# Slots in four operations with the sum of the ranks in PSUM, and new orders of the engines, in an attention and mixture-of-experts kernel

## The reference

```python
def _L0_attn_ref(x, w_qkv, w_swiglu, w_out):
    qkv = jnp.einsum('btd,ed->bte', rms_norm(x), w_qkv)
    q, k, v = jnp.split(qkv, 3, axis=-1)
    q = rms_norm(q); k = rms_norm(k)
    w = jnp.exp(k)
    kv = jnp.cumsum(w * v, axis=1)
    w = jnp.cumsum(w, axis=1)
    y = jax.nn.sigmoid(q) * kv / (w + 1e-06)
    u, g = jnp.split(jnp.einsum('bte,fe->btf', y, w_swiglu), 2, axis=-1)
    return x + jnp.einsum('btd,ed->bte', u * jax.nn.silu(g), w_out)
...
        mask = jax.nn.one_hot(top1, e, dtype=jnp.int32)
        ranks = jnp.cumsum(mask, axis=0) - 1
        mask = mask * (ranks < capacity).astype(jnp.int32)
...
    h = _layernorm(x, axis=-1) * (1 + ca) + sa
    x = x + ga * _L0_attn_ref(h, L0_attn_w_qkv, L0_attn_w_swiglu, L0_attn_w_out)
    h = _layernorm(x, axis=-1) * (1 + cb) + sb
    x = x + gb * _L0_ffn_ref(h, L0_ffn_gate_w, L0_ffn_w1, L0_ffn_w2)
```

## Time and profile before

| what | value |
|---|---|
| median of 3 runs | 208.44 us (207.78 to 210.2) |
| the profiled execution | 208.38 us, span 206.2 us |
| mean granted TensorE clock | 0.979 |
| TensorE busy | 191.4 us (93%) |
| VectorE busy | 151.9 us (74%) |
| ScalarE busy | 145.0 us (70%) |
| GpSimd busy | 122.5 us (59%) |

### The profile page before, as it was taken

The page is one execution under the profiler, slowest core; times in us unless marked ns, Lnnn a source line. Parts: engine busy times, 40 slices in busy tenths (PEclk is TensorE's granted clock), DMA queues, the critical chain, the costliest instruction groups (busy, mean ns, idle before and its releaser), DMA issues.

```text
span 206.2 us, 4074 instructions
## 1 busy us (share of the span) xinstructions
PE 191.4 (93%) x1189; PEld 156.6 (76%) x1189; DVE 151.9 (74%) x475; ACT 145.0 (70%) x424; POOL 122.5 (59%) x154
## 2 busy tenths in 40 slices
PE   7999999999999989998868999999999999999970
PEld 4789778788898868775665668897988879787950
DVE  2678999999999999999974675274857756685530
ACT  4587999999999979886566654585674858553400
POOL 6232744356378887577776781415775845586674
PEclk9978999999999999999996999999999999999998
DMA  4999999999401413232399564997859575410000
GB/s 134 285 331 358 359 356 340 282 343 289 141 3 51 154 56 115 89 118 77 114 307 395 213 164 146 342 319 248 264 174 354 175 240 170 147 48 30 34 30 14
DMA packets 38596, 40.25 MB, mean 195 GB/s; under 512 B 2623, under 2 KB 32646, under 8 KB 38576
## 3 DMA queue, kind: packets, MB, share of 16 engines
q1 hardware_dynamic: 35248, 32.94, 51.6%
q0 software_dynamic: 3328, 7.07, 9.5%
HBM read 19.85 MB, written 19.94 MB: 193 GB/s over the span
## 4 chain that ended last, share of the span: by engine, by line
PE 65%; DVE 16%; ACT 6%; issue 5%; POOL 3%; DMA 2%; POOLq 1%; DVEq 0%; ACTq 0%
PE bank L1352 15%; PE bank L1338 12%; PE bank L1105 4%; POOL out_dram L568 3%; PE bank L1123 3%; PE bank L1158 2%; PE bank L1144 2%; PE bank L1160 2%; PE bank L1116 2%; PE bank L1287 2%; ACT junk L599 2%; PE bank L1212 2%; PE bank L1095 2%; PE bank L1175 2%; PE bank L1309 2%
## 5 line engine op out<-in xcount | busy, mean ns | idle before, releaser
L568 POOL DMA_INDIRECT out_dram<-x_all,rest x40 | 42.8, 1069 | 26.4 <-DVE x_all L1051 13.7
L531 POOL DMA_INDIRECT dispatched_rows<-rows,slot x32 | 32.5, 1015 | 12.3 <-issue 8.1
L748 ACT ACTIVATE HT<-bank 128x320 f32<-128x320 f32 x64 | 28.0, 438 | 10.6 <-PE bank L1338 10.2
L1352 PE MATMUL bank<-HT,w 128*128 128x320 f32 x112 | 32.4, 432 | 0.0
L1352 PEld LDWEIGHTS bank<-HT,w 128*128 128x128 f32 x112 | 20.6, 189 | 6.7
L1338 PE MATMUL bank<-xth,w1h 128*128 128x320 f32 x64 | 22.5, 351 | 0.0
L1338 PE MATMUL bank<-xtl,w1h 128*128 128x320 f32 x64 | 19.8, 309 | 0.0
L1338 PE MATMUL bank<-xth,w1l 128*128 128x320 f32 x64 | 19.8, 309 | 0.0
L1070 DVE COPY OT<-bank 128x320 f32<-128x320 f32 x14 | 6.9, 491 | 16.2 <-PE bank L1352 16.2
L599 ACT ACTIVATE junk<-bank 128x128 f32<-128x128 f32 x64 | 16.7, 306 | 1.2 <-PE bank L1105 1.1
L306 POOL TENSOR_SCALAR xh<-x_all,rs,nm 128x128 f32<-128x128 f32 x24 | 10.4, 448 | 11.0 <-DVE nm L778 11.0
(11 more groups left out here) (179 smaller groups left out, 504.1 us busy)
## 6 DMA issues: line engine op xcount, KB each, us to landing
dispatched_rows<-blank SPq DMA_DIRECT2D x9, 965.0 KB, 13.3
w<-in_L_ffn_w_dram SPq DMA_DIRECT2D x16, 512.0 KB, 7.7
rest<-dispatched_rows SPq DMA_DIRECT2D x8, 645.0 KB, 5.7
hin<-dispatched_rows SPq DMA_DIRECT2D x7, 320.0 KB, 6.2
x_all<-in_L_attn_x_dram SPq DMA_DIRECT2D x8, 256.0 KB, 5.1
rows<-gb_row SPq DMA_DIRECT2D x8, 256.0 KB, 4.0
out_dram<-rows SPq DMA_DIRECT2D x8, 256.0 KB, 4.0
x_all<-dispatched_rows SPq DMA_DIRECT2D x1, 645.0 KB, 4.7
```

The source lines that it names most:

```text
L531: pool.indirect_dma_start(out=disp_d, out_offset=bass.IndirectOffsetOnAxis(ap=slot[:, b, j:j + 1], axis=0), in_=rows[:, b, j, :], in_offse ...
L568: pool.indirect_dma_start(out=out_d.rearrange("b t d -> (b t) d"), out_offset=bass.IndirectOffsetOnAxis(ap=rest[i % RING][:, n, C_TOK - D: ...
L748: act.activation(HT[e][:, f, :], ps_h[c % HB][:, 0:CAP], ACT.Gelu_apprx_tanh).then_inc(h_done, 1)
L1352: last = pe.matmul(ps_o[e], w2[i % RING][:, e, f, :], HT[e][:, f, :], start=(f == 0), stop=(f == NF - 1))
```

## The change

`slots` loses sl_o and gets four operations. The reversed expert numbers `rev` are now multiples of 320, negative (so `best` is a minimum), and `seen` starts at a negative constant, so that the ranks come out as the rank less the capacity. The sum goes to PSUM (`ps_sums`: four columns of bank "t" for blocks 0 to 3, of bank "v" for blocks 4 to 7). sl_a adds best, a constant and the sum; slot is the larger of sl_a and the sum times a large number, which sends tokens beyond the capacity out of bounds. The claims on TensorE follow: `ranks` holds "t" until slot_done for blocks 0 to 3, and "v" until slot_done for blocks 4 to 7.

All four lists are laid out anew. These steps change their engine: modulate1(6) and modulate2(6) from ScalarE to VectorE, normalize2(3) from ScalarE to GpSimd, normalize2(7) from ScalarE to VectorE; weigh_sums 0, 4 and 7 are on VectorE instead of 1 and 3; silu 0, 1 and 7 instead of 1, 6 and 7, the others on GpSimd. One run_late(384) is left out at the end of TensorE's list. The diff, with the lists cut to the start and the end:

```diff
@@
-            pool.memset(seen[:, :, :], 0.0).then_inc(pool_setup, 1)
-            pool.iota(rev_i[:, :], pattern=[[0, NJ], [-1, NE]], base=NE, channel_multiplier=0
+            pool.memset(seen[:, :, :], -CAP / (P * NJ)).then_inc(pool_setup, 1)
+            pool.iota(rev_i[:, :], pattern=[[0, NJ], [CAP, NE]], base=-NE * CAP, channel_multiplier=0
...
-            squares(0); normalize1(pool, 1); squares(1); normalize1(pool, 3); squares(2)
-            weigh_sums(pool, 0); squares(3); normalize1(pool, 4); silu(pool, 0); number_slots()
...
+            squares(0); normalize1(pool, 1); squares(1); normalize1(pool, 3); squares(2); squares(3)
+            normalize1(pool, 4); weigh_sums(pool, 1); squares(4); normalize1(pool, 5); number_slots()
...
+            weigh_sums(pool, 5); normalize2(pool, 3); scatter(1); weigh_sums(pool, 6); silu(pool, 5)
+            count_seen(2); scatter(2); silu(pool, 6); count_seen(3); scatter(3); count_seen(4); scatter(4)
+            count_seen(5); scatter(5); count_seen(6); scatter(6); scatter(7)
...
-            ln2_scale(6); h2_rows(act, 5); exp_logits(5); normalize2(act, 6); modulate2(act, 6)
-            ln2_scale(7); exp_logits(6); normalize2(act, 7); h2_rows(act, 6); modulate2(act, 7)
-            h2_rows(act, 7); exp_logits(7)
...
+            ln2_scale(6); normalize2(act, 6); h2_rows(act, 5); ln2_scale(7); exp_logits(6)
+            modulate2(act, 7); h2_rows(act, 6); exp_logits(7); h2_rows(act, 7)
@@
-                dve.tensor_reduce(best[:, b, :], cand[:, :, :], X, ALU.max).then_inc(best_done, 1)
+                dve.tensor_reduce(best[:, b, :], cand[:, :, :], X, ALU.min).then_inc(best_done, 1)
@@
-                dve.tensor_reduce(rank[:, :], rk[:, :, :], X, ALU.add).then_inc(rank_done, 1)
+                dve.tensor_reduce(ps_sums[b // FIRST], rk[:, :, :], X, ALU.add).then_inc(rank_done, 1)
                 dve.wait_ge(rank_done, b + 1)
-                dve.scalar_tensor_tensor(sl_a[:, :], best[:, b, :], -float(CAP), rank[:, :], ALU.mult, ALU.add)
-                dve.tensor_scalar(sl_o[:, :], rank[:, :], float(CAP), float(NOWHERE), ALU.is_gt, ALU.mult
-                                  ).then_inc(sl_done, 1)
+                dve.scalar_tensor_tensor(sl_a[:, :], best[:, b, :], float((NE + 1) * CAP - 1), ps_sums[b // FIRST],
+                                         ALU.add, ALU.add).then_inc(sl_done, 1)
                 dve.wait_ge(sl_done, b + 1)
                 if b < NB - 1:
-                    dve.scalar_tensor_tensor(slot[:, b, :], sl_a[:, :], float(NE * CAP - 1), sl_o[:, :],
-                                             ALU.add, ALU.add).then_inc(slot_done, 1)
+                    dve.scalar_tensor_tensor(slot[:, b, :], ps_sums[b // FIRST], float(SKIP), sl_a[:, :],
+                                             ALU.mult, ALU.max).then_inc(slot_done, 1)
...
             stats1(3); modulations(); diagonal(0); weigh_v(0); normalize1(dve, 2); aggregate1(3)
-            h_means(1); qk_means(1); scan_w(0); shift1(3); modulate1(dve, 2); denominator(0); scan_kv(0)
-            weigh_v(1); stats1(4); aggregate1(4); h_means(2); qk_means(2); modulate1(dve, 3); clamp_g(0)
...
+            h_means(1); qk_means(1); scan_w(0); modulate1(dve, 2); shift1(3); denominator(0); weigh_v(1)
+            scan_kv(0); stats1(4); weigh_sums(dve, 0); aggregate1(4); modulate1(dve, 3); h_means(2)
...
-            stats2(6); gate_u(7); aggregate2(6); top_value(5); shift2(6); top_expert(5); top_prob(5)
-            slots(5); residual(7); stats2(7); aggregate2(7); top_value(6); shift2(7); top_expert(6)
...
+            top_value(5); top_expert(5); top_prob(5); shift2(6); residual(7); slots(5); stats2(7)
+            aggregate2(7); modulate2(dve, 6); shift2(7); normalize2(dve, 7); top_value(6); top_expert(6)
             top_prob(6); slots(6); top_value(7); top_expert(7); top_prob(7); slots(7); last_slots(7)
             hot_slots()
@@
-                claim(pe, "t", rk_done, b)
+                claim(pe, "t", slot_done if b < FIRST else rk_done, b)
+                if b >= FIRST:
+                    claim(pe, "v", slot_done, b)
...
             transpose1(0); weights_over(); run_early(1); project_qk(0); h_square_sums(0)
-            modulation_products(); transpose1(1); run_early(2); project_v(0); project_qk(1)
-            h_square_sums(1); transpose_k(0); transpose_q(0); transpose1(2); project_v(1); transpose_kv(0)
-            row_product(0); project_qk(2); transpose_k(1); h_square_sums(2); transpose1(3); project_g(0)
...
+            modulation_products(); transpose1(1); run_early(2); transpose_q(0); project_qk(1)
+            transpose_k(0); project_v(0); h_square_sums(1); transpose1(2); transpose_kv(0); project_v(1)
+            row_product(0); transpose1(3); project_qk(2); transpose_kv(1); h_square_sums(2); project_g(0)
...
-            h2_back(5); logits(5); project_out(7); ranks(5); transpose2(6); logits(6); run_late(384)
-            h2_back(6); run_late(384); ranks(6); transpose2(7); run_late(256); logits(7); h2_back(7)
-            run_late(384); ranks(7); run_late(384); run_late(384); run_late(384)
...
+            transpose2(5); project_u(7); logits(5); project_out(7); ranks(5); h2_back(5); transpose2(6)
+            run_late(384); logits(6); h2_back(6); transpose2(7); run_late(384); ranks(6); logits(7)
+            run_late(256); run_late(384); ranks(7); h2_back(7); run_late(384); run_late(384)
```

112 lines of the change are left out of this document (55 added, 57 removed).

## The result

The changed kernel takes 211.82 us (median of 4 runs, 211.08 to 212.34), the kernel before 208.34 us beside it. The ratio is 1.0157 with a 95% interval of 1.0093 to 1.0220: slower by 1.6%. The forecast was 207.5 us in a range of 204.7 to 210.9, so the time lies 0.9 us outside. What happened is the rival that ended on the other side, "TensorE does not get its 3.5 us back", which was put at 211.0 us.

What follows compares the result with a forecast made beforehand. TensorE and VectorE were taken as both nearly full for the first 100 us. VectorE's losses and gains nearly cancel up to residual(7), the tail brings far_rows 0.9 us earlier: 208.38 - 0.9 = 207.5 us, range 204.7 to 210.9.

Steps and rivals of the forecast that it cites:

- TensorE does not get its 3.5 us back: Slower rival: TensorE, 3.5 us late from the start, uses under about 1 us of 2.44 us room: 211.0 us, chance 0.15.
- The slots: VectorE's slot operations: stalls worth 3.8 us go, dropping sl_o saves 0.5 us, writing PSUM costs no more.
- the rivals without effect and with dear operands: Slots on VectorE: still blocking on SBUF, 210.8 us, chance 0.05; PSUM operands dearer, 208.4 to 209.3 us, chance 0.05.
- The start: First block: weigh_v(0) waits for the later project_v(0), idling VectorE 3.2 us; project_qk(2) at 26.9, TensorE 3.5 us late.
- its own sign of being wrong: TensorE's clock: the prediction is wrong if another half-rate stretch appears between 20 and 30 us.
- VectorE's ledger to residual(7): VectorE up to residual(7): +3.2 start, +0.8, +0.65, -3.8 stalls, -0.5 sl_o, -0.8 slots(5), from 105.84 to 105.4.
- The balance: VectorE's gains and losses up to residual(7) nearly cancel and the tail gives 0.9 us: 207.5 us, chance 0.47.
- Bank holds: Banks "t" and "v" stay claimed until slot_done: nothing charged, at most 4 x 0.6 us.
- GpSimd's silu and normalize2: GpSimd gets normalize2(3) and silu(6) ahead of scatters: nothing, unless expert loads come later than the second pair's work.
- ScalarE's relief: ScalarE loses two modulations and two normalize2 of 1.63 us: nothing credited directly.
- The tail: From residual(7) on: normalize2(7) ends after 4.6 us, slot(6) at 112.7 to 113.6, far_rows 0.9 us earlier (0.5 to 1.4).
- The limit that was named: Before far_rows: the load behind slot(6) leaves no spare; rows land at 123.3 to 124.2, so far_rows waits for them.

Runs made afterwards that it cites:

- project_v(0) first: Changed kernel with project_v(0) put back ahead of transpose_q(0) on TensorE, nothing else: 207.61 us, ratio 0.9942.
- the slots alone: Kernel before with its own four lists of steps and only the new slots: 205.08 us, ratio 0.9842.
- project_v(0) late: Kernel before with project_v(0) moved behind project_qk(1) and transpose_k(0) on TensorE: 212.74 us, ratio 1.0255.
- the gaps filled: Unread matmuls put into TensorE's gaps, in the changed kernel (212.49 us, ratio 1.0129) and in project_v(0) late (211.87 us, 1.0180).

## Why the prediction was wrong, step by step

*The slots.* Right. The stalls of sl_a and slot are gone, the write into PSUM costs 8 ns (228 for 220), and sl_a and slot are no dearer than their floor of 161; the rivals without effect and with dear operands are out. Alone the step takes 3.65 us off VectorE's work, for 4.3 forecast, of which 2.99 show at residual(7) and 1.6% in the time. The rule weighed there from the Trainium skill ("SBUF — State Buffer", Who interferes with whom) agrees with the 157 to 159 ns; the estimate of 1.5 us from the table in "VectorE: DVE Perf Modes" (The TRN2 errata) does not show.

*The start.* Right in its mechanism, and at weigh_v(0) in its size; too small on TensorE. weigh_v(0) was put at 19.7 and came at 20.73, but 0.82 us of its lateness stems from steps that both kernels share: the change cost 3.4 us there for 3.2 forecast. project_qk(2) was put at 26.9, 4.0 us late (3.5 with the transpose taken off that it has done by then). It came at 28.53, 5.6 us late, and ended 6.9 us late, since it took 3.24 us instead of about 2. The prediction named the two holes and the possible half-rate stretch, and left the stretch in the rival instead of in the sum; its own sign of being wrong, such a stretch between 20 and 30 us, came. The step by itself is worth 4.2 us by the medians in the new orders and 4.6 us in the old ones (4.5 and 5.3 by the ratios); the intervals reach down to the forecast 3.5, so the times do not show that it was too small.

*VectorE's ledger to residual(7).* This step failed. It set -3.8 (stalls) -0.5 (sl_o) against +0.8 and +0.65 for the work moved to VectorE, -0.8 for slots(5), and so expected the stretch from weigh_v(0) at 89.33 - 3.65 = 85.7 us. It took 90.15. The run with project_v(0) first isolates the step: there the stretch still took 89.17, and residual(7), which the prediction put near 102.2 without the late start, came at 106.37 (0.7 of that was there at weigh_v(0)). Two things were missing. The moved operations were priced at the duration they have alone, and it was not asked which other operations with both inputs in SBUF would now start beside GpSimd: yT(7) took 2.02 for 0.67, three nrm 0.83 to 1.01 for 0.16, and one nm 0.89 for 0.15. VectorE won the stalls of the slots and lost as much on others, 4.1 us for 3.8. And the ledger counted VectorE only. TensorE's work in the stretch is 84 to 85.6 us in every kernel of the two tables; in the new orders it stands idle 4.7 us even with project_v(0) first, with the slots alone 1.9. Relieving VectorE alone returned about a third of the relief or less (0.52 of 1.43, 0.39 of 1.52). How the missing 3.5 us divide between the two, the runs leave open.

*The balance.* "Lost and won nearly cancel" was therefore wrong by 5.5 us at residual(7): 105.4 forecast, 110.88 found, of which 1.0 was there at weigh_v(0) (0.8 of it from the shared steps), some 3.5 are the ledger's, and 1.0 is what the late start cost behind weigh_v(0). The condition under which the slower rival decides, that less than 1 us of the room is used, was given as "VectorE's own waits fall elsewhere". That is what they did.

*Bank holds, TensorE's other order, GpSimd's silu and normalize2, ScalarE's relief.* Little or nothing of these shows. TensorE's longest waits in the stretch are for xh(3), yT(7) and a GT; the one wait for a slot ahead of a transpose, slot(3), is 0.3 us, as one for rk is.

*The tail.* The number came, -1.16 us from residual(7) to near_rows in the trace for -0.9 forecast, but in part by luck. VectorE's steps went much as forecast: normalize2(7) took 1.11 us for 1.15, transpose2(7) went at once (115.69, xh2(7) at 115.47), slot(6) was done at 118.63, 7.75 us after residual(7) began. But the 7.3 to 8.2 us forecast for slot(6) were those at full and at half clock; 7.75 was found at full clock, and 8.8 to 8.9 in the two traces where it fell. By the traces the gain of about 1.1 us goes with the clock that stays at 1.00 behind residual(7), which the forecast knew only as a bound on slot(6); where it fell, far_rows was no nearer to residual(7) than in the kernel before (18.93 and 18.98 us for 18.75). The limit that was named did show: in six of the other traces with this tail far_rows waits 0.2 to 0.6 us for its load. Put on the slots alone the tail brought 0.84 us by the medians, within the noise.

## What to carry to other kernels

A stall that comes from sharing is no property of the operation that shows it: before counting it as won, list which operations of the new order can start beside the other engine's, and price moved work with that stall and without. Where two engines are both nearly full, the ledger of one does not give the length of the stretch; look at the idle time of the other and what ends it. Where the clock differs between two traces, compare a stretch only with one at the same clock. When an order is laid out anew, the first block's critical step deserves its own line in the sum: here one step of 128 on TensorE decided the sign.

## What the runs showed of the hardware

- A small operation with its inputs in SBUF can stand behind several GpSimd operations in a row: 4.14 us for four elements, to within 0.03 us of the end of the fourth after the one it met. With one operand in PSUM no stall was seen: 157 to 159 ns for all eight, of which three lay beside xh or gs of GpSimd, which read SBUF (with the slots alone, four of eight beside xh or yT).
- GpSimd is held up as well: seen took 0.77 us behind yT(7) instead of 0.30.
- One tensor operand is not enough to be safe: tensor_scalar from SBUF to SBUF of 128x2 took up to 999 ns beside GpSimd.
- Stretches of some 3 us at half clock come and go in the first stage. Behind gaps of TensorE (1.3 and 1.5 us) the granted clock was 0.50 from 28 to 30 us in the changed kernel, and behind others (1.9 and 1.3 us) 0.56 and 0.58 from 22 to 26 in the kernel before with project_v(0) late; with the gaps filled it was 1.00, in one trace of each. But from 12 to 20 us four traces have such a stretch and others with the same list up to there have none, so the gap alone is not shown to be the cause.
